# Cross-attention: the queries' trailing bits in tiles of 128 rows, half of them zero

## The reference, cut to what matters

```
q = split_heads(layernorm(x) @ Wq.T + bq)          # [b, 16, 100, 16]
k = split_heads(context @ Wk.T + bk)               # [b, 16, 361, 16]
v = split_heads(context @ Wv.T + bv)
scores = einsum('bhqd,bhkd->bhqk', q, k) / sqrt(16)
scores = where(mask == 0, -inf, scores)
out = einsum('bhqk,bhkd->bhqd', softmax(scores), v)
x = x + merge_heads(out) @ Wo.T + bo
```

## Time and profile before

| | us |
|---|---|
| median of 3 runs | 2038.47 |
| lowest, highest | 2029.75, 2044.36 |
| span of the profiled execution | 2060.8 |
| of it cross-attention (first to last shifted matmul) | 856.2 to 1639.4 |

### The profile page before, as it was taken

One profiled execution on the slowest core, in us unless ns is written; L12 is line 12 of the kernel. 1 busy time (PEld: TensorE's weight loads), 2 busy tenths in 40 slices (PEclk: granted clock), 3 DMA queues, 4 the chain that ended last, 5 costly groups with the idle time before them and its releaser, 6 DMA issues. The chain is left out here.

```text
span 2060.8 us, 41207 instructions
## 1 busy us (share of the span) xinstructions
PE 1873.6 (91%) x12756; PEld 1524.5 (74%) x12756; DVE 1206.7 (59%) x3493; ACT 830.0 (40%) x1768; POOL 641.2 (31%) x844
## 2 busy tenths in 40 slices
PE   2999999999999999799999999999999960799998
PEld 2788888888797978577777777777777660688887
DVE  4765647474656554366666666666666531455554
ACT  3544535353545443244444444444444410122221
POOL 1202020202011101344444444444444316233332
PEclk9996969696969796699999999999999955899999
DMA  8302020111102020200000000000000015345552
GB/s 230 82 1 65 7 57 15 48 28 36 43 20 56 7 64 1 67 21 21 20 20 20 20 25 24 21 20 20 20 20 10 2 42 146 107 162 197 172 175 87
DMA packets 119659, 113.34 MB, mean 55 GB/s; under 512 B 57559, under 2 KB 108503, under 8 KB 119352
## 3 DMA queue, kind: packets, MB, share of 16 engines
q1 hardware_dynamic: 113784, 101.90, 17.2%
q0 software_dynamic: 3968, 6.59, 1.0%
q10 hardware_dynamic: 1856, 4.19, 0.6%
HBM read 87.71 MB, written 26.90 MB: 56 GB/s over the span
## 5 line engine op out<-in xcount | busy, mean ns | idle before, releaser
L1050 DVE CUSTOM_DVE_ANT_0 masked<-psb_s,mask_f 100x361 f32<-100x361 f32 x512 | 265.6, 533 | 197.6 <-PE psb_s L1181 188.7
L940 ACT ACTIVATE probs<-psb_t,key_bias 121x400 f32<-121x400 f32 (+1 forms) x384 | 228.6, 595 | 343.5 <-PE psb_t L1196 342.7
L379 POOL TENSOR_TENSOR diag<-neg_ident,row_max 100x400 fp32r<-100x400 f32 x128 | 106.7, 855 | 464.1 <-PE ps_t L612 320.5
L871 POOL TENSOR_TENSOR diag<-neg_ident,row_max 100x400 fp32r<-100x400 f32 x128 | 111.5, 871 | 365.9 <-DVE row_max L1050 365.9
L1181 PE MATMUL psb_s<-k_both,qd_hi 128*100 128x362 f32 x512 | 178.5, 360 | 1.4 <-DVE row_max L1050 1.4
L1192 PE MATMUL psb_t<-qd_hi,k_both 128*121 128x400 f32 (+1 forms) x384 | 171.6, 447 | 0.0
L1190 PE MATMUL psb_t<-qd_lo,k_both 64*121 64x400 f32 (+1 forms) x384 | 170.1, 443 | 0.0
L1841 PE MATMUL psd_h<-h_in,w_sb 128*128 128x256 f32 x640 | 144.2, 384 | 1.4 <-ACT h_in L1707 1.4
L1849 PE MATMUL psd_y<-w_sb,hid 128*128 128x256 f32 x640 | 144.5, 379 | 0.0
L1841 PEld LDWEIGHTS psd_h<-h_in,w_sb 128*128 128x128 f32 x640 | 123.5, 193 | 19.0 <-issue 1.8
L1196 PE MATMUL psb_t<-diag,ones_r 100*121 100x400 f32 (+1 forms) x384 | 134.2, 350 | 0.3 <-POOL diag L871 0.3
(11 more groups left out here) (229 smaller groups left out, 4469.3 us busy)
## 6 DMA issues: line engine op xcount, KB each, us to landing
w_sb<-in_w SPq DMA_DIRECT2D x40, 1024.0 KB, 7.6
v_rows<-v_tok SPq DMA_DIRECT2D x32, 400.0 KB
v_ext<-v_rows SPq DMA_DIRECT2D x32, 400.0 KB
c_tok<-in_context SPq DMA_DIRECT2D x32, 242.0 KB
routed_rows<-empty SPq DMA_DIRECT2D x1, 5140.0 KB, 21.3
rows<-routed_rows SPq DMA_DIRECT2D x20, 257.0 KB, 8.2
mask_i<-in_mask SPq DMA_DIRECT2D x32, 141.0 KB
c_tok<-in_context SPq DMA_DIRECT2D x32, 119.0 KB
```

The lines of the kernel that those rows point to most:

```text
L379: pool.tensor_tensor(diag[:, g % 2], c.neg_ident[0:S, 0:S].unsqueeze(1).to_broadcast([S, GH, S]), row_max[:, g // 2 % 2, g % 2].unsqueeze( ...
L871: pool.tensor_tensor(diag[:, u % 2], c.neg_ident[0:S, 0:S].unsqueeze(1).to_broadcast([S, 4, S]), row_max[:, u % 2].unsqueeze(2).to_broadca ...
L940: act.activation(probs[0:KT[kt], u % 2, kt], ps_t[i % 2][0:KT[kt], 0:4 * S], ACT.Exp, bias=bias, scale=HD2 ** -0.5).then_inc(probs_ready, 1)
L1050: dve.tensor_tensor_reduce(masked[:, h % 2], ps_s[h % 2][0:S, 0:S2], mask_f[:, p], 1.0, -3.0e38, ALU.add, ALU.max, row_max[:, (h // 4) % 2 ...
```

## The change

`qd_lo` gets a tile of 128 rows for every quarter instead of one for every pair. For quarter u=2g+a, rows 64a to 64a+63 hold the trailing bits as before and the other 64 rows are zero. The zero rows are written once, by two memsets on GpSimd at the start of the stage. All 128 rows of `k_both` enter the first matmul of `shifted`, as they do the second; the zero rows cancel the half that holds the keys' trailing bits.

On GpSimd, `place` writes the trailing bits with two multiplications of 64 rows by 400 instead of one of 128 by 400, each of them behind a wait for the multiplication before it (semaphore `place_step`), and signals `qd_ready` once at its end, by 3.

```diff
-        qd_lo = sb("qd_lo", [128, 2, KD, 4, S], F32R)
+        qd_lo = sb("qd_lo", [128, 2, 4, 4, S], F32R)
+        place_step = sem("place_step")
...
             pool.memset(v_ext[:, :, :, :, HD2:32], 0.0).then_inc(pad_ready, 1)
-            pool.wait_ge(pad_ready, 3)
+            for a in range(2):
+                pool.wait_ge(pad_ready, 3 + a)
+                pool.memset(qd_lo[64 - 64 * a:128 - 64 * a, :, a::2].bitcast(F32), 0.0).then_inc(pad_ready, 1)
+            pool.wait_ge(pad_ready, 5)
...
                 for u in (2 * g, 2 * g + 1):
-                    pool.tensor_tensor(qd_hi[:, pp, u], q_hi[:, u:u + 1, :].to_broadcast([128, 4, S]), own,
-                                       ALU.mult).then_inc(qd_ready, 1)
-                pool.tensor_tensor(qd_lo[:, pp, g], q_lo[:, g:g + 1, :].to_broadcast([128, 4, S]), own,
-                                   ALU.mult).then_inc(qd_ready, 1)
+                    ins = pool.tensor_tensor(qd_hi[:, pp, u], q_hi[:, u:u + 1, :].to_broadcast([128, 4, S]), own,
+                                             ALU.mult)
+                ins.then_inc(place_step, 1)
+                for a in range(2):
+                    half = slice(64 * a, 64 * a + 64)
+                    pool.wait_ge(place_step, pb * 6 + (3 * g + 1 + a))
+                    pool.sem_inc(pool_passed, 1)
+                    ins = pool.tensor_tensor(qd_lo[half, pp, 2 * g + a], q_lo[half, g:g + 1, :].to_broadcast([64, 4, S]),
+                                             c.head_of[half].unsqueeze(2).to_broadcast([64, 4, S]), ALU.mult)
+                    ins.then_inc(place_step, 1)
+                pool.wait_ge(place_step, pb * 6 + (3 * g + 3))
+                pool.sem_inc(qd_ready, 3)
...
-            pe.wait_ge(pad_ready, 3)
+            pe.wait_ge(pad_ready, 5)
...
-                rows, half = slice(KT0[kt], KT0[kt] + n), slice(64 * (u % 2), 64 * (u % 2) + 64)
+                rows = slice(KT0[kt], KT0[kt] + n)
                 out = ps_t[i % 2][0:n, 0:4 * S]
-                pe.matmul(out, k_both[half, p, u, rows], qd_lo[half, p, u // 2].rearrange("p h s -> p (h s)"),
+                pe.matmul(out, k_both[:, p, u, rows], qd_lo[:, p, u].rearrange("p h s -> p (h s)"),
                           start=True, stop=False)
```

## The result

| | before | changed |
|---|---|---|
| median, us | 2041.41 (4 runs) | 2084.86 (4 runs) |
| lowest, highest | 2029.75, 2060.49 | 2066.0, 2094.16 |
| span of the profiled execution | 2060.8 | 2078.3 |

The ratio is 1.0227 with a 95% interval of 1.015 to 1.0304: 2.3% slower. Run again on another occasion it was 1.0166 [1.0064, 1.0269]. I had forecast 1998 us, 40 less, with 1952 to 2028 as range; both the sign and the range were wrong.

A forecast was written before the change was run, and what follows sets the result against it. TensorE, at full clock, was taken to bound cross-attention, with GpSimd setting each step's second half afterwards: 13.33 + 9.92 = 23.25 us, 1.24 less, 38 us in 31 steps, plus 2, so 40 less: 1998 us, range 1952 to 2028.

The forecast's parts named there:

- What bounds the kernel, part 1: Cross-attention's shifted tiles: TensorE bounds the stage; a first matmul over 128 rows removes row changes, 0.37 us a tile.
- uncovered loads stay: Rival, 8%: equal rows leave TensorE's weight loads uncovered, so the change saves nothing there; 14 us slower, 2052.
- Matmul saving, a step: TensorE's work in a cross-attention step: 11 x 0.37 + 0.19 = 4.26 us less, 136 us over 384 tiles.
- the first half: Step from L1196 of tile (3,0) to the queries: 11.66 us before, 9.25 after savings, 9.92 with new waits of 0.67.
- TensorE's side of the second: Queries to L1196 of (3,0): TensorE's own work 10.98 us, plus 0.9 of ScalarE and VectorE delays, hidden behind GpSimd's 13.33.
- Part 2, price of a multiplication: GpSimd's place: each multiplication costs 0.855 us whatever its rows, eight of them instead of six.
- the rival at 1955: Rival, 8%: GpSimd's pieces scale with rows, place takes 5.56 us, a step 21.8, 83 us less in all.
- Part 2, price of a wait: GpSimd's place: six waits for its own results at 0.084 us each, making place 7.26 us, 2.35 more.
- my upper bound: GpSimd's place with each wait at 0.17 us: 7.8 us in all.
- Who waits, first half: L1196 of (3,0) to queries: TensorE saves 2.41 us, new waits cost 0.67, so 11.66 becomes 9.92.
- The sum: Steps of 23.25 us, 1.24 less, 31 times: 38 us, plus 2 for the last step; 40 us less, 1998.
- The one on the slower side: Rival, 7%: GpSimd's place becomes the bound while TensorE saves nothing, waits at 0.17; 0.95 us a step, 2068.

The follow-up runs named there:

- the filled kernels: Changed kernel with the first matmul of tile (3,0) made eight or four times more ahead of the real one, overwritten; ratios to before 0.9928 and 0.9909.
- place alone: Changed kernel, but the first matmul of a shifted tile over 64 rows again; ratio to the kernel before 1.0384.
- changed, filled with four: Changed kernel with four additional, overwritten matmuls ahead of the real first one of tile (3,0); ratio to the kernel before 0.9909.
- no count: Changed kernel without the increment of pool_passed between place's waits and the multiplications behind them; ratio to the kernel before 0.9866.

## Why the prediction was wrong

*What bounds the kernel, part 1.* Right. TensorE paid for the change of rows, 0.37 us a tile was to go, and 1.10 became 0.71. The rival "uncovered loads stay" is refuted by the load of L1204 under a matmul of the same rows, and with it, for this kernel, the rule of the Trainium skill that stood behind it ("TensorE: Matmul & The Clock Gate", Part 3).

*Matmul saving, a step.* Right where it can be seen alone: I had 9.92 for the first half and 10.98 + 0.9 for TensorE's side of the second; measured 9.92 and 11.82.

*Part 2, price of a multiplication.* Right: 0.85 at 64 rows, so the rival at 1955 falls.

*Part 2, price of a wait.* Mis-sized. I took 0.084 from L838 and L840 for all six. The rows of L838 and L840 have a wait and then the instruction; place has an increment between. Measured 0.18 at five of them and 0.32 behind the last; the 0.17 of my upper bound was the better price, though even its 7.8 was exceeded. Place was 7.94, not 7.26, and the queries stood 0.11 further ahead of it: 14.11 instead of 13.33, 0.78 a step. Alone that would have left a step of 24.03; the filled kernels show 24.13, 0.35 under before.

*Who waits, first half.* This is the step that failed. I let the wait of "about 2 us" cost its own length and kept every TensorE distance at the full clock, from a stage that showed 1.00 while TensorE was busy 299.98 of 300 us. The clock falls around the end of the wait, and 9.92 became 11.4. Shown by filling the wait: 1.35 us a step, 36 us. In the prediction's terms: 23.25 + 0.78 + 1.35 = 25.4; measured 25.5.

*The sum.* Thirty steps are 0.9 us longer in the mean, 27 us; the stage of the two profiles is only 16.7 longer, because its two ends are 10 shorter together. Of these, 6.7 lie ahead of the first tile (3,0), and not all of them are the change's merit: in the kernel before that stretch took 26.0 us at clock 0.65 (857.4 to 883.4), in the changed kernel 19.3 at 1.00 (858.2 to 877.5). So part of these 6.7 us belongs to the clock in that one execution of the kernel before, and the 16.7 us understate the loss. The medians lie 43 apart. The repeat, with a stage of 809.2, shows that the clock's falls differ from execution to execution; how the remaining difference splits is not resolved.

*Rivals.* The one on the slower side named the right place, L1196 of (3,0), and nearly the right price of a wait, but not the cause: it had TensorE save nothing. That its direction came true is luck. I had written that with the saving real GpSimd would have to lose 1.9 us a step more to get there; it lost 0.78, and the clock took 1.35. No rival had the clock in it.

**Open:** what decides whether the clock falls. A fall came with idle time of 1.02 us before L1208 in every step (place alone), with 1.4 us in the first step alone (changed, filled with four), with 1.75 in six of thirty (no count), with 2.1 in 26 of thirty (changed). The length of that wait alone does not order these four, and in the last two kernels the same wait is followed by a fall in some steps and not in others.

## What to carry to other kernels

Where a saving on TensorE opens a wait of a microsecond or two in a loop, do not price the wait at its length: look for the clock behind it, and take a stretch at 1.2 GHz in each pass as a rival case; here it mostly lasted 3.4 us and cost 1.35 to 1.6 us. Before adding work to an engine that is half idle, find the instruction behind which it is put and who waits for that; here the same four multiplications, without any wait of their own, cost 0.94 us a step more ahead of the diagonal than behind it (22.79 against 21.85). Take the price of a wait from a row with the same instructions around it, not just from the same engine.

## What the runs showed of the hardware that was not expected

- Around the end of 1 to 2 us without matmuls, from 0.3 us before TensorE resumed to 2 us after it, a stretch of mostly 3.4 us began with a granted clock near half (0.50 from 1050.2 to 1053.6 in the changed kernel); useless matmuls in the gap prevented it (0.94 to 1.00 over 600 us) and made two kernels faster by 36 and 46 us of stage.
- A GpSimd instruction behind a wait for the one before it started 0.08 us after that one's end, and 0.18 with a semaphore increment in between.
- GpSimd's multiplication of 64 rows by 400 took 0.85 us, as long as that of 128 rows.
